# Causal mask of the maxima pass on VectorE, output rescaling moved, all groups in one sequence

## The reference, cut to what matters

```python
h = _layernorm(x, axis=-1) * (1 + ca) + sa
qkv = h @ Wqkv                                   # x: (2, 2048, 256)
q = qkv[..., :2 * Hx].reshape(Bx, 2 * NQ, Sx, HD)   # NQ = 16, HD = 16
k = qkv[..., 2 * Hx:2 * Hx + G].reshape(Bx, NKV, Sx, HD)   # NKV = 8
v = qkv[..., 2 * Hx + G:].reshape(Bx, NKV, Sx, HD)
scores = einsum('bhqd,bhkd->bhqk', q, repeat(k)) / sqrt(HD)
scores = where(causal, scores, -inf)
aw = softmax(scores, axis=-1).reshape(Bx, NQ, 2, Sx, Sx)
aw = aw[:, :, 0] - lam * aw[:, :, 1]
attn = einsum('bhqk,bhkd->bhqd', aw, repeat(v)) * (1.0 - LAMBDA_INIT)
```

## Time and profile before

| | us |
|---|---|
| median of 3 runs | 2430.19 (2429.91 to 2431.61) |
| the profiled execution's own time | 2430.3 |
| its span, first to last instruction | 2428.4 |
| one group in the middle, from first exponential to the next one's | 114.9 |
| group 15, which has only 17 steps' worth of units | 92.0 |
| units ahead of group 0 | 57.3 |
| behind the attention | 486.4 |

### The profile page before, as it was taken

One profiled execution on the slowest core, in us unless ns is written; L12 is line 12 of the kernel. 1 busy time (PEld: TensorE's weight loads), 2 busy tenths in 40 slices (PEclk: granted clock), 3 DMA queues, 4 the chain that ended last, 5 costly groups with the idle time before them and its releaser, 6 DMA issues. The chain is left out here.

```text
span 2428.4 us, 46606 instructions
## 1 busy us (share of the span) xinstructions
PE 2220.2 (91%) x17772; PEld 992.5 (41%) x17772; DVE 1829.4 (75%) x3782; ACT 1547.9 (64%) x3105; POOL 525.7 (22%) x584
## 2 busy tenths in 40 slices
PE   6799999999999999999999999999999979889984
PEld 4233333333333333333333333334333258567831
DVE  2788888878787888888888888887888348434467
ACT  2167677777767776767676777777767725235633
POOL 2112121303222121212121213131201014100067
PEclk8589999999999999999999999999999979899955
DMA  4120302121121202020303030212100030000001
GB/s 145 36 58 6 66 11 61 22 50 32 41 41 31 47 25 47 30 56 17 66 6 66 6 66 18 55 27 45 32 12 2 2 96 0 1 1 1 1 22 48
DMA packets 95990, 84.79 MB, mean 35 GB/s; under 512 B 48544, under 2 KB 81440, under 8 KB 95776
## 3 DMA queue, kind: packets, MB, share of 16 engines
q1 hardware_dynamic: 95776, 81.91, 15.2%
HBM read 26.81 MB, written 16.78 MB: 18 GB/s over the span
## 5 line engine op out<-in xcount | busy, mean ns | idle before, releaser
L605 DVE TENSOR_REDUCE m_part<-a_bank 128x1 f32<-128x512 f32 (+3 forms) x2560 | 1395.5, 603 | 270.0 <-PE a_bank L906 163.2
L749 ACT ACTIVATE probs<-b_bank 128x512 f32<-128x512 f32 (+1 forms) x2304 | 1173.2, 578 | 412.4 <-PE b_bank L922 407.2
L922 PE MATMUL b_bank<-q_pack,k_pack 34*128 34x512 bf16 (+7 forms) x5120 | 949.0, 348 | 6.2 <-DMA q_pack<-m_rows 1.8
L894 PE MATMUL a_bank<-k_pack,q_pack 64*128 64x512 bf16 (+3 forms) x2560 | 847.2, 357 | 58.5 <-DVE m_part L605 33.0
L960 PE MATMUL acc<-probs,v_tile 128*32 128x512 f32 (+3 forms) x5120 | 587.1, 540 | 22.6 <-ACT o_sb L756 21.5
L922 PEld LDWEIGHTS b_bank<-q_pack,k_pack 34*128 34x128 bf16 (+1 forms) x5120 | 316.5, 94 | 547.7 <-ACT probs L749 392.6
L894 PEld LDWEIGHTS a_bank<-k_pack,q_pack 64*128 64x128 bf16 x2560 | 238.2, 94 | 333.4 <-DVE m_part L605 255.2
L476 POOL TENSOR_SCALAR_AFFINE_SELECT probs<-probs 128x512 f32<-128x512 f32 (+1 forms) x192 | 151.5, 789 | 1019.4 <-ACT probs L749 1019.4
L906 PE MATMUL a_bank<-future,pick 64*128 64x128 bf16 x2048 | 278.3, 219 | 0.0
L906 PEld LDWEIGHTS a_bank<-future,pick 64*128 64x128 bf16 x2048 | 185.7, 96 | 47.5 <-issue 4.7
L960 PEld LDWEIGHTS acc<-probs,v_tile 128*32 128x32 f32 x5120 | 107.3, 108 | 186.6 <-issue 94.2
(11 more groups left out here) (193 smaller groups left out, 1761.0 us busy)
## 6 DMA issues: line engine op xcount, KB each, us to landing
q_pack<-part SPq DMA_DIRECT2D x384, 64.0 KB, 2.3
k_pack<-part SPq DMA_DIRECT2D x192, 64.0 KB, 2.3
scratch<-qkv_row SPq DMA_DIRECT2D x16, 512.0 KB, 2.8
heads<-scratch SPq DMA_DIRECT2D x16, 512.0 KB, 3.7
xg<-in_L_attn_x SPq DMA_DIRECT2D x16, 256.0 KB, 2.8
scratch<-qkv_row SPq DMA_DIRECT2D x32, 128.0 KB, 2.7
q_pack<-m_rows SPq DMA_DIRECT2D x256, 2.0 KB
x<-in_L_attn_x SPq DMA_DIRECT2D x4, 1024.0 KB, 11.7
```

What stands on the lines that cost most here:

```text
L605: dve.tensor_reduce(m_part[:, 2 * hp + side, t, c:c + 1], a_bank[at % A_RING][:, 0:width_a(u % UNITS)], AX.X, ALU.max).then_inc(a_maxed, 1)
L749: act.activation(probs[:, s % P_RING, h, at:C], b_bank[bank_no(("B", par, s, h))][:, at:C], ACT.Exp, scale=HD ** -0.5) \
L894: ins = pe.matmul(a_bank[at % A_RING][:, 0:w], q_pack[buf][rows, hp, 0, q:q + P], k_pack[buf][rows, 0, C * c:C * c + w], start=True, stop= ...
L922: ins = pe.matmul(b_bank[bank_no(slot)][:, at:at + C - q], k_pack[par][rows, n2, P * kt:P * (kt + 1)], q_pack[par][rows, h // 2, n2, C * j ...
```

## The change

- The mask matmuls L906 and their constants go. On a tile of the diagonal DVE's fused operation adds `mask_a` (0, and minus 3e38 over the triangle) to the bank, writes the bank back and takes the maximum. One call of it is two instructions on DVE: the main one and one that writes the accumulated value to `m_part`.
- The three operations behind a block's last unit are spread over the next unit's two tiles. `m_part` has two buffers.
- Output: ACT copies the turned rows from the bank to `o_rows`; DVE inverts and multiplies the signs a step later, apart from each other; the product with the rows is POOL's.
- The gather of heads goes from DVE (step 15) to POOL (step 14), T0 to T3 one step later, M one step later.
- The extra uses of a bank stand between heads 1 and 2 of a step, on PE and on ACT, and `take_output` too.
- No flush: V of steps 34 and 35 is met in steps 0 and 1 of the next group, block 3's copy and O in its steps 1 and 2. The loop runs over 576 steps and three more.

```diff
+LAST_STEP = STEPS * GROUPS
-PREP_AT = {7: "N", 8: "W0", 9: "W1", 10: "W2", 11: "W3", 17: "T0", 18: "T1", 19: "T2", 20: "T3"}
+PREP_AT = {7: "N", 8: "W0", 9: "W1", 10: "W2", 11: "W3", 18: "T0", 19: "T1", 20: "T2", 21: "T3"}
+COPY_AT = {STEPS * g + J_LAST[j] + LAG: 4 * g + j for g in range(GROUPS) for j in range(NJ)}
+OUTPUT_AT = {n + 1: block for n, block in COPY_AT.items()}
+MAXIMA_AT = {n + 2: 4 * (u // UNITS) + A_LAST.index(u % UNITS)
+             for n in range(LAST_STEP) for u in units(n) if u % UNITS in A_LAST}
...
+            def pair(n):
...
+                pool.wait_ge(o_weighed, n + 1)
+                if n:
+                    pool.wait_ge(o_added, n)
+                pool.tensor_tensor(o, o_rows[:, :].rearrange("p (t h e) -> p t h e", t=TB, h=QH)[:, :, :, 0:HD],
+                                   o_w[:, :, :].unsqueeze(3).broadcast_to([P, TB, QH, HD]), ALU.mult).then_inc(o_scaled, 1)
+                pool.wait_ge(o_scaled, n + 1)
+                pool.tensor_tensor(dst, halves[:, :, :, 0, :], halves[:, :, :, 1, :], ALU.add).then_inc(o_added, 1)
...
+            def maximum(u, n):
...
+                if c == j:
+                    dve.tensor_tensor_reduce(out=bank[:, 0:w], in0=bank[:, 0:w], in1=mask_a[:, C - w:C], scale=1.0, scalar=NEG,
+                                             op0=ALU.add, op1=ALU.max, accum_out=out).then_inc(a_maxed, 1)
+                else:
+                    dve.tensor_reduce(out, bank[:, 0:w], AX.X, ALU.max).then_inc(a_maxed, 1)
...
+            def unit_maxima(u, last):
...
+                maximum(u, 0)
+                if before is not None:
+                    negate(before)
+                maximum(u, 1)
+                if before is not None:
+                    negate_rest(before)
+                if m is not None:
+                    block_maximum(u, m)
...
+            for n in range(TAIL):
+                g, s = n // STEPS, n % STEPS
+                ahead = list(units(n)) if n < LAST_STEP else []
+                for k, u in enumerate(ahead):
+                    unit_maxima(u, u == UNITS * GROUPS - 1)
+                    if k == 0 and n - 1 in OUTPUT_AT:
+                        invert(OUTPUT_AT[n - 1])
...
+                if n - 1 in OUTPUT_AT:
+                    weigh(OUTPUT_AT[n - 1])
...
+            def take_rows_of_output(block, no, bank):
+                act.wait_ge(misc_filled, no)
+                if block:
+                    act.wait_ge(o_added, block)
+                act.activation(o_rows[:, :], bank[:, :], ACT.Copy).then_inc(o_taken, 1)
...
-            def mask_head(i, par, u, n):
...
-                if c == j:
-                    for m in range(2):
-                        ins = pe.matmul(a_bank[at % A_RING][:, w - P:w], pick[rows, m, :], future[rows, m, :], start=False, stop=m == 1)
-                    ins.then_inc(a_scored, 1)
...
+                if n < LAST_STEP:
+                    two_heads(n, 0, share(ahead, 0, 2))
+                if LAG <= n < LAST_STEP + LAG:
+                    meet_v(n - LAG)
+                for use in uses_at(n):
+                    wait_for_bank(use)
...
+                if n < LAST_STEP:
+                    two_heads(n, 1, share(ahead, 1, 2))
```

More of the change, by code:

```diff
@@ L635, in _ @@
[L635 to L636 removed]
+                unit_maxima(u, False)
             def gates():
```

497 lines of the change are left out of this document (204 added, 293 removed).

## The result

The changed kernel takes 2441.5 us, the median of six runs (2438.6 to 2450.1), against 2430.9 of six runs of the kernel before beside them: ratio 1.0046, 95% interval 1.0030 to 1.0063. It is slower by some 11 us; I had forecast 2380, with a range of 2290 to 2480, and faster as the likely direction.

The account below looks back on a forecast made before the run. PE and DVE, handing three banks to and fro, were taken to stall each other. Terms summed to -3.1 us a group: -47 over 15 groups, +1 for one without the gather, -4 for group 15, so -50: 2380, range 2290 to 2480.

Parts of the forecast that it names:

- my cases: Whole kernel: forecast 0.48, looser PE-DVE coupling 0.20, accumulator read not overlapped 0.22, half rate 0.03, nothing moves 0.07.
- fused operation: Maxima pass on DVE: second instruction on 64 tiles a group, 0.12 us each at weight 0.8, +6.1 us a group.
- mask matmuls: Maxima pass on PE: removing them wins 1.5 us by waits to 3.5 if all streamed; taken as -2.2 a group.
- gather: DVE at step 15: 0.82 us of work and 0.9 of DMA wait go, -1.4 us in each of 14 groups.
- output's large product off VectorE: Output rescaling: the product moves to POOL, costing it about half of 1.29 us; part of the -4.6 a group.
- negated maxima: DVE behind a block's last unit: three dependent operations fall from 0.56 to about 0.28 us interleaved, -0.9 us a group.
- the rest: Per group: O's wait for PE, 0.81 us each, within output rescaling's -4.6; ACT's cast +0.5, copies covered; no flush -0.6.
- output rescaling: At each group's four O's: DVE's 1.66 us of wait and operations becomes 0.2, at weight 0.8, -4.6 us a group.
- The rival that charged the unoverlapped read: Diagonal tiles on DVE: each ends in a full wait, 0.26 us instead of 0.12, +115 us, 2495; chance 0.22.
- the half rate: Diagonal tiles on DVE: the fused operation runs at half rate, another 0.33 us each, +273 us, 2653; chance 0.03.
- My low end: Fused mask on DVE: the second instruction costs 0.08 us, a little less than a small instruction's 0.09; 4.1 us a group.
- my signs of being wrong: Fused pair over 0.18 us more than a plain one, a changed plain step, or PE's attention clock not 1.00.

Follow-up runs that it names:

- both masks: Mended kernel with the mask matmuls back on PE and the fused operation adding zeros; 2401.4 us.
- mask on PE: Mended kernel with the two mask matmuls per diagonal tile back on PE and plain reductions on VectorE; 2381.6 us.
- mended: Changed kernel with POOL's subtractions behind step 27, block 2's row maxima ahead of the packing, head transposes one step earlier; 2344.4 us.
- gather back: Mended kernel with the gather of heads back on VectorE behind step 15; 2360.7 us.
- product back: Mended kernel with the output's large product back on VectorE; 2366.2 us.
- turned as before: Mended kernel with the row maxima negated in three operations together and turned one step behind the block's last unit; 2356.1 us.
- the last run: Mended kernel with ACT's cast of the head block behind all four exponentials of step 20, not between their halves; 2342.3 us.
- the last two runs: Two runs against the mended kernel: row maxima negated and turned as before, 2356.1 us; cast behind all four exponentials of step 20, 2342.3 us.

## Why the prediction was wrong

The direction was wrong. The time was inside the range by luck: none of my cases has the mechanism that made it. By its own terms, over the whole kernel:

| term | forecast, us | measured, us | from |
|---|---|---|---|
| fused operation | +98 | +20 | both masks against mask on PE |
| mask matmuls | -35 | -57 | both masks against mended |
| gather | -20 | -16 | gather back |
| output's large product off VectorE | -26 | -22 | product back |
| negated maxima | -14 | -12 | turned as before |
| the rest: O's wait for PE, ACT's copies and cast, flush | -53 | 0 | mended with the mask on PE against before (-50), less the three above |
| `o_w` under POOL's subtraction, maxima behind the packing, copies and cast in step 21, with the clock's falls behind them | 0 (the cast's +7 is in the row above) | +97 | mended against changed |

The forecast column adds up to -50, the measured one to +10, which is the result. The measured terms were taken out one at a time, so what two of them share falls to the rest.

**The failing step** is in output rescaling: "Now two small operations stand apart among tiles whose inputs have long been there: 0.2", and with it "The product costs POOL about half of 1.29 us; POOL is busy 24.2 of 114.9 and nobody waits for `attn`". I looked at POOL only as a receiver of work, by its busy share. It has three subtractions of 4.07 us, and a VectorE product that meets one waits for its end: `o_w` took up to 3.29 us where I charged 0.2 for two such operations, and taking the meeting away won 35.6 us. The trace before had the sign, though I showed no row of it: an `o_w` of 0.91 where its like take 0.17. The move put it 0.8 or 2.3 us behind the start of a subtraction, where it had been 0.9 ahead of the end of one.

**The second** is a queue that I didn't follow: I took the flush as a matter of PE and VectorE alone (-1.9 at its step and -0.8 for O's wait there, +1.3 for V in steps 0 and 1; measured -2.9 and +1.2 over steps 0 to 2), but the packing on SP waits for that V and the maxima's rows stand behind the packing. 28 us.

**The third** I saw and undersized: "Its cast of a whole head block now stands in a step of four full exponentials: I charge +0.5". It was 1.8 us a group by the steps 17 to 23 of the changed and the mended kernel, and 0.7 of that is step 23, where the clock fell in seven of 14 groups. The cast's place within step 20 is not it (the last run shows that). That it is the cast together with a copy of 1.02 ahead of full exponentials is my reading of the view above: the run that moved them moved all four transposes, so no run separates cast, copy and transposes.

**The mask** was mis-sized in my disfavour. The price of the pair, 0.12 with bounds 0.08 to 0.26, was 0.02 to 0.05 measured start to start, and 1.2 us a group over all, where I had +6.1. For the mask matmuls I gave -3.5 "if all 32 units streamed on the path" and took -2.2, nearer VectorE's waits; 3.2 was measured in a middle group, near the end that I didn't take. The rival that charged the unoverlapped read is out, and so is the half rate. My low end was the smallest spacing that I saw between a small VectorE instruction and the next; a read that follows its own main operation turned out to be cheaper than that.

**The clock.** "PE's granted clock in the attention isn't 1.00" was among my signs of being wrong, and it came, in two places. In step 26 it was 0.60 to 0.72 in the seven groups where PE had stood for 2.3 us, and 1.00 in the seven where it had stood for 0.8 to 0.9. In step 23 it was 0.65 in the other seven, behind a stand of 0.98 in step 22 that all 14 groups have; what sets one half apart from the other the traces don't show. In the run with the subtractions moved step 26 has 1.00 everywhere, and with the transposes earlier step 23 has too. The fall isn't a cause of its own but makes such a stand dearer: step 26 takes 4.0 to 4.5 with it and 2.95 without, step 23 4.8 and 3.27. By these lengths the falls are some 20 us of the 97, an estimate.

**What held.** The predicted lengths of steps 5 and 35, and of step 23 in half of the groups; steps without anything special at 2.50 (steps 14 to 16; but step 32, which I had named as the plain one, took 2.67, and the one ahead of it 0.30 less than before); and the prices of gather and product to within 5 us each, that of the negation for a partly different reason. I said 111.8 for a middle group. Groups 1 to 13 of the changed kernel take 115.2 to 119.1, those of the mended one 110.0.

**What stays open.** The rest term: O's wait, ACT's copies and the flush together are worth nothing net, where I had some 50 us, although the 10.3 us by which `o_w` was held before are gone as well. The gains at steps 5, 23, 24 and 35 are there (-1.2, -0.6, -0.8, -2.9 against before in the mended kernel), and steps 0 to 2, 9 and 20 to 22 lose 1.2, 0.45 and 1.1. For steps 20 to 22 the later turn of the maxima and the cast's place are excluded by the last two runs, and the fused mask by the mended kernel with the mask on PE (9.63 there); no run tells what it is. Giving back the flush by itself was not tried.

## What to carry to other kernels

Before a small VectorE product or copy between SBUF tiles is moved, look at what POOL runs at its new time: not POOL's busy share but the length of its longest instruction, and whether instances of the same line already differ in length in the trace at hand. Read it over all groups: in group 9 step 23 had its gain, in seven others not. When a dependency moves by two steps, follow it into every queue that waits for it, and read what stands behind the waiting entry. And when a change of several parts comes out near zero, look for its parts by step: here a gain of 87 us and a loss of 97 lay on top of one another, and three moves of a line or two each kept the gain.

## What the runs showed of the hardware

- A VectorE product (two SBUF sources) or copy times a number (one) of 128x16 fp32, 0.17 us by itself, lasts until a running POOL subtraction ends: up to 3.29 us. POOL's mask of `probs` holds such an operation in the same way (0.76 for 0.17). A reciprocal of the same size in the same place takes 0.25, and none of some 330 plain reductions from PSUM that were issued inside a POOL instruction was longer.
- The fused add and max with its accumulator read costs 0.02 us (128 and 512 columns) to 0.05 us (256 and 384) more from start to start than the plain reduction of as many elements, though its read shows 0.14.
- Two mask matmuls of 128 columns per tile cost 3.2 / 64 = 0.05 us a tile in a middle group, about what one of the two streams: in the trace before two of them start 0.05 apart.
- After PE had stood for 2.3 us its clock was granted at 1.2 GHz for a time (3.4 us in group 9), in seven of seven groups of the changed kernel and ten of 13 of the run with block 2's maxima first, at a place where it otherwise keeps 2.4 GHz. In the changed kernel it was so after a stand of 0.98 us in seven of 14 groups, after one of 0.8 to 0.9 in none of seven.
